# Eight float PSUM banks become six float and two bfloat16 ones in a two-layer transformer kernel

## The chip, the cores and the metric

The kernel runs on one Trainium2 chip, on its 8 cores, each core working on one of 8 sequences with no exchange between them. The time is device microseconds of the slowest core. Times of single executions of the kernel before were 11906.31 and 11831.79 us, median 11869.05 us.

## The reference

Two transformer layers over x of shape (8, 2048, 1024), each of an attention-like part and a feed-forward part, every part followed by a residual sum and a layer norm:

```python
x = L0_attn_x
x = _layernorm(x + _L0_attn_ref(x, ...), axis=-1)   # RWKV: k, v, r projections, scan over time, output projection
x = _layernorm(x + _L0_ffn_ref(x, ...), axis=-1)    # 1024 -> 4096 -> 4096 -> 4096 -> 1024, ternary weights
x = _layernorm(x + _L1_attn_ref(x, ...), axis=-1)   # gated linear attention, 4 heads, 8-bit/ternary quantised linears
x = _layernorm(x + _L1_ffn_ref(x, ...), axis=-1)    # 1024 -> 4096, depthwise conv over 3, silu, 4096 -> 1024, quantised
```

The part on which the change bears most is the recurrence of the gated linear attention:

```python
def step(S, inp):
    qt, kt, vt, gt = inp
    S = jnp.exp(gt)[..., None] * S + kt[..., None] * vt[..., None, :]
    o = jnp.einsum('bhk,bhkv->bhv', qt, S)
    return (S, o)
```

## The kernel before, in words

Each core keeps its sequence transposed in SBUF as `XA` (128 partitions, 8 channel groups, 2048 tokens, float). The program is a list of operations written out by hand, one list for each engine (`t` TensorE, `v` VectorE, `s` ScalarE, `g` GpSimd, `y` SyncE). `P.op(engine, fn, after=[...])` appends an operation and the tokens it waits for; an engine works through its list strictly in the order in which the list was written, so an operation that waits holds up all behind it. Waits become semaphore waits. The order in which the loops emit operations is therefore the order of the work.

PSUM is used as eight tensors `PS[0]` to `PS[7]`, each one bank (128 x 512 float). `PSB[b]` is the same bank b seen as 128 x 1024 bfloat16 by a bitcast. `bank_free[b]` holds the token of the last read of bank b.

The stages in order:

- `_emit_prepass`: reads the weights of layer 1, takes the mean magnitude (a matmul with ones into `PS[7]`, `t_scale`, L408), quantises them and writes them back to DRAM. It is spread in small pieces over the stages up to the first layer norm.
- `stage_l0attn`: banks 0 to 4.
- `stage_ln` (4 times): for 16 tiles of 128 tokens, 8 transposes into banks 5 and 6 (L643), two ScalarE copies out of them, statistics, and for the first three norms 8 transposes back through banks 3 and 4.
- `stage_l0ffn`: two halves of 1024 tokens. Phase A: for 32 output blocks j, 16 matmuls with `w1R` and 16 with `w2R` (L775) into four banks; Silu of the first pair on ScalarE (L785), its product with the second pair on VectorE (L795). Output block j uses banks (j % 2) * 2 + {0, 1} and 4 + (j % 2) * 2 + {0, 1}: two sets of four, in turn. There are two weight buffers; both loads of block j + 1 are issued by GpSimd when the last matmul of block j is done. Phases B and C (L823): 64 matmuls for each of 32 blocks, banks 4 to 7 in two pairs in turn, Gelu on ScalarE (L834). Then `w3R` (L860), banks 0 to 3 in two pairs.
- `stage_l1attn`: 8 blocks of 256 tokens. Transposes of x through banks 5 and 6 (L962), five quantised projections (their operand transposed as bfloat16 through banks 5 and 6, L1037, and matmuls into banks 0 to 3), then two chunks of 128 tokens with 4 heads each, then the output projection `owT` (L1397). One head of one chunk is the piece that matters here, 8 x 2 x 4 = 64 times:
  - VectorE ends its preparation with f7 (`KG`, L1240);
  - TensorE forms the 128 x 128 scores in `PS[2]` (`amm`, L1247, two matmuls of float, four instructions); VectorE masks them out of there into `A2` (`aev`, L1251);
  - TensorE transposes `KG` into `PS[4]` (`ktp`, L1257, two transposes); VectorE copies that to `KGt` (`kev`, L1260);
  - TensorE forms the output in `PS[3]` (`omm`, L1267 from the state S, then L1271 from `A2`) and the state's increment in `PS[6]` and `PS[7]` (`dmm`, L1276);
  - VectorE updates S (`su`, L1282, twice) and gates the output (`oev`, L1288); the next head's first operation on ScalarE (f1, L1215) waits for that.
- `stage_l1ffn`: 4 quarters of 512 tokens. Each quarter starts with 4 tiles: T(tt), 8 transposes of x into banks 5 and 6 (L1595), two VectorE copies (L1599, L1601), quantisation, and, one tile behind, S2(tt - 1), 8 bfloat16 transposes into banks 5 and 6 again (L1503) with two VectorE copies (L1509). Then matmuls with `f1T` (L1638) into banks 0 and 1, the convolution, a maximum over transposes through `PSB[5]` (L1683), small transposes through `PS[6]` (L1703), quantisation, matmuls with `f2T` (L1740) into banks 2 and 3.

Of the kernel before, what the change touches and what calls it, by code (L numbers as in the profile page):

```python
# [9 lines left out]
BF16 = mybir.dt.bfloat16  # L10
AF = mybir.ActivationFunctionType
ALU = mybir.AluOpType
AXX = mybir.AxisListType.X
# [185 lines left out]
def build(upto="all", tap=None):  # L199
# [47 lines left out]
    with ExitStack() as es:  # L247
# [4 lines left out]
        P = Prog(nc, sems)  # L252

        def sb(name, shape, dt=F32, stack=None):
# [11 lines left out]
              for b in range(8)]  # L266
        PSB = [PS[b][:, :].bitcast(BF16) for b in range(8)]
# [100 lines left out]
def _emit_prepass(P, pre, din, qscr, SCL, ONES, PS, d_ones):  # L368
# [4 lines left out]
    for nm, di, do in QW:  # L373
        wi = QWI[nm]
# [32 lines left out]
        def t_scale(wi=wi, inv_n=inv_n):  # L407
            mm = P.op("t", lambda t: t.matmul(  # L408
                PS[7][:, 0:1], ONES[:], pre["acc"][:, :], start=True, stop=True),
                after=[state["g"], d_ones, state["tread"]])  # L410
            state["tread"] = P.op("v", lambda v: v.tensor_scalar(
                SCL[:, wi:wi + 1], PS[7][:, 0:1], inv_n, 1e-5,
# [202 lines left out]
def stage_ln(ctx, which, toks):  # L615
# [5 lines left out]
    with ExitStack() as st_:  # L621
# [12 lines left out]
        for tt in range(NTT):  # L634
# [4 lines left out]
            for c in range(NC):  # L639
                bank = 5 + c // 4  # L640
# [7 lines left out]
                tmb[:, 0:512], PS[5][:, :], AF.Identity), after=[tps[3], stt, tm_free[sl]])  # L648
            e2 = P.op("s", lambda s, tmb=tmb: s.activation(
                tmb[:, 512:1024], PS[6][:, :], AF.Identity), after=[tps[7], e1])  # L650
# [64 lines left out]
def stage_l0ffn(ctx, toks, debug_stop=None):  # L715
# [3 lines left out]
    with ExitStack() as st_:  # L719
# [31 lines left out]
        for hb in range(2):  # L751
# [10 lines left out]
            for j in range(32):  # L762
# [19 lines left out]
                for s2 in range(2):  # L782
                    scj = j
                    bank = (j % 2) * 2 + s2
# [21 lines left out]
            for phase, nm, scoff, SRC, DST in (  # L806
                    ("B", "h1R", 64, H0, H1X), ("C", "h2R", 96, H1X, H0)):
                for j in range(32):
# [21 lines left out]
                    for s2 in range(2):  # L830
                        off = s2 * 512
                        bank = 4 + (j % 2) * 2 + s2
# [50 lines left out]
def stage_l1attn(ctx, toks):  # L883
# [6 lines left out]
    with ExitStack() as st_:  # L890
# [62 lines left out]
        for blk_i in range(8):  # L953
            t0 = blk_i * 256
            for tt in range(2):
                tps = []
                for c in range(NC):
                    bank = 5 + c // 4
# [6 lines left out]
                for half in range(2):  # L965
                    bank = 5 + half
# [155 lines left out]
            for tt in range(2):  # L1122
# [47 lines left out]
                    PSB[2][0:16, 0:128], QSz[:, 0:16], IDB[:]), after=[u7, bank_free[2]])  # L1170
                zb_free[0] = tp
                ev = P.op("v", lambda v, tt=tt: v.tensor_copy(
                    X2Q[:, tt * 128:(tt + 1) * 128], PSB[2][0:16, 0:128]),
                    after=[tp, vt])
                vt = ev
                bank_free[2] = ev
# [24 lines left out]
            for cn in range(2):  # L1201
# [12 lines left out]
                for h in range(4):  # L1214
# [49 lines left out]
                    bank_free[4] = kev  # L1264
# [10 lines left out]
                    for j in range(2):  # L1275
                        dmm.append(P.op("t", lambda t, h=h, cn=cn, j=j: t.matmul(  # L1276
                            PS[6 + j][:, :], KGt[:, j, :],
                            V[:, cn, h * 512:(h + 1) * 512],
                            start=True, stop=True),
                            after=[kev, bank_free[6 + j]]))  # L1280
                    for j in range(2):
                        su = P.op("v", lambda v, h=h, j=j: v.scalar_tensor_tensor(  # L1282
                            S[:, 2 * h + j, :], S[:, 2 * h + j, :],
                            DC[:, 2 * h + j:2 * h + j + 1], PS[6 + j][:, :],
                            ALU.mult, ALU.add), after=[dmm[j], omm, dc1, vt])
                        vt = su
                        bank_free[6 + j] = su
# [230 lines left out]
def stage_l1ffn(ctx, toks):  # L1518
# [5 lines left out]
    with ExitStack() as st_:  # L1524
# [52 lines left out]
        for q in range(4):  # L1577
# [8 lines left out]
            for tt in range(4):  # L1586
# [3 lines left out]
                for c in range(NC):  # L1590
                    bank = 5 + c // 4
# [292 lines left out]
```

How the kernel before makes its waits and increments, by code:

```python
            def body(eng):  # L145
                seen = {}
                for i, rec in enumerate(prog.ops[e]):
                    for kind, val in rec["waits"]:
                        if seen.get(kind, 0) >= val:
                            continue
                        eng.wait_ge(prog.sems[kind], val)
                        seen[kind] = val
                    inst = rec["fn"](eng)
                    if rec["dma"] is not None:
                        inst.then_inc(prog.sems[rec["dma"]], 16)
                    amt = incs[e].get(i)
                    if amt:
                        inst.then_inc(prog.sems[e], amt)
```

## Time and profile before

| | |
|---|---|
| median of 2 runs | 11869.05 us (11831.79 to 11906.31) |
| the profiled execution | 11890.16 us |
| its span (slowest core, core 7) | 11888.6 us |
| spans of all cores | 11784.2 to 11888.6 us |
| busy: TensorE (PE), VectorE (DVE), ScalarE (ACT), GpSimd (POOL) | 5393.1, 3384.1, 1840.5, 387.2 us |
| share of the span | 45%, 28%, 15%, 3% |
| the chain that ended last, by engine | PE 42%, DVE 24%, DMA 19%, issue 7%, ACT 6% |
| HBM | 70 GB/s over the span |

How to read it: the profile was taken in one execution, which was 21 us above the median of the two timed ones. Its span runs from the first to the last instruction of the slowest core. An engine's busy share is an average over stages whose limits differ. The chain that ended last is followed back from the last instruction, at each step to what released it. In the views quoted below PE is TensorE's matmuls, PEld its weight loads (which may run under the matmuls before them), and L1257 is line 1257 of the kernel.

### The profile page before, as it was taken

The page shows a single profiled execution, that of the slowest core. Times are in us where ns is not written, and L with a number is a line of the kernel's source. Part 1 is how long each engine was busy: PE and PEld are TensorE (multiplying, and loading weights), DVE is VectorE, ACT ScalarE, POOL GpSimd, SP SyncE. Part 2 cuts the span into 40 slices and gives each one's busy share as a digit, 9 for nine tenths or more (in the row PEclk, how much of TensorE's full clock was granted, in tenths as well). Part 3 has the DMA queues.
Part 4 walks back from the last instruction along what each step waited for, and adds up shares of the span by engine and source line. Part 5 has one row for each costly group of instructions (what it writes and reads, how often), then busy time and mean ns, then how long its engine had stood idle before and what let it go on. Part 6 is the DMA issues. An engine that isn't in the chain of part 4 may idle for free.

```text
span 11888.6 us, 72155 instructions; the slowest of 8 cores (11784.2 to 11888.6 us)
## 1 busy us (share of the span) xinstructions
PE 5393.1 (45%) x22678; PEld 2580.6 (22%) x22678; DVE 3384.1 (28%) x5916; ACT 1840.5 (15%) x2558; POOL 387.2 (3%) x777
## 2 busy tenths in 40 slices
PE   3430006666666666666663333333333333324323
PEld 1120002222222222222222222222222222112112
DVE  6762231000000100000004444444434434453453
ACT  1222101000000000000003122122122223121121
POOL 0000110000000000000000000000000000000000
PEclk7665558888888788878786666666666666657656
DMA  4223432222222222222211111111201101011012
GB/s 117 74 76 112 135 117 39 41 43 43 43 43 45 38 41 43 43 39 43 43 36 57 36 54 61 53 37 61 68 37 60 60 22 34 28 30 57 26 31 80
DMA packets 169144, 637.24 MB, mean 54 GB/s; under 512 B 24832, under 2 KB 25216, under 8 KB 157504
## 3 DMA queue, kind: packets, MB, share of 16 engines
q0 software_dynamic: 81088, 237.61, 10.7%
q1 hardware_dynamic: 87680, 395.02, 10.0%
q8 instruction: 187, 3.06, 0.1%
q14 instruction: 189, 1.55, 0.0%
HBM read 794.50 MB, written 42.01 MB: 70 GB/s over the span
## 4 chain that ended last, share of the span: by engine, by line
PE 42%; DVE 24%; DMA 19%; issue 7%; ACT 6%; DVEq 1%; POOL 1%; ACTq 0%; SPq 0%; POOLq 0%
PE ps L823 17%; PE ps L775 5%; DMA f_wj<-h1R 4%; DMA f_wj<-h2R 4%; PE ps L1740 2%; PE ps L1100 2%; PE ps L860 2%; DMA f_wj<-w1R 2%; PE ps L1638 2%; PE ps L1267 2%; PE ps L1397 2%; DMA pre_in<-f1T 1%; DMA pre_in<-f2T 1%; PE ps L1081 1%; DMA b_wj<-q_f2T 1%
## 5 line engine op out<-in xcount | busy, mean ns | idle before, releaser
L823 PE MATMUL ps<-f_h,f_wj 128*128 128x512 bf16 x8192 | 2059.6, 419 | 1122.6 <-DMA f_wj<-h1R 561.4
L823 PEld LDWEIGHTS ps<-f_h,f_wj 128*128 128x128 bf16 x8192 | 865.6, 106 | 2316.6 <-issue 1582.3
L871 DVE SCALAR_TENSOR_TENSOR XA<-ps,SVEC,XA 128x512 f32<-128x512 f32 x32 | 24.0, 751 | 3549.6 <-PE ps L860 3547.3
L775 PE MATMUL ps<-f_h,f_wj 128*128 128x512 bf16 x2048 | 579.6, 453 | 525.6 <-DMA f_wj<-w1R 518.6
L834 ACT ACTIVATE f_h<-ps,f_sc 128x512 bf16<-128x512 f32 x256 | 176.4, 689 | 2957.1 <-PE ps L823 2944.9
L1740 PE MATMUL ps<-b_hc,b_wj 128*128 128x512 bf16 x1024 | 293.4, 457 | 486.7 <-DVE b_hc L1472 360.6
L775 PEld LDWEIGHTS ps<-f_h,f_wj 128*128 128x128 bf16 x2048 | 230.6, 113 | 874.1 <-issue 721.3
L1100 PE MATMUL ps<-a_wl,a_xqf 128*128 128x512 bf16 x1024 | 294.9, 458 | 143.3 <-DMA a_wl<-q_vwT 63.8
L795 DVE SCALAR_TENSOR_TENSOR f_h<-ps,f_sc,f_g 128x512 bf16<-128x512 f32 x128 | 96.1, 751 | 783.1 <-ACT f_g L785 776.4
L860 PE MATMUL ps<-f_h,f_wj 128*128 128x512 bf16 x1024 | 255.5, 416 | 139.2 <-DMA f_wj<-w3R 139.2
L1247 PE MATMUL ps<-a_qg,a_kp 128*128 128x128 f32 x256 | 76.3, 454 | 524.0 <-DVE a_kg L1240 524.0
L1683 PE MATMUL ps<-c_idb,b_hc 128*128 128x128 bf16 x512 | 75.1, 302 | 523.8 <-ACT b_hc L1666 397.8
L535 PE MATMUL ps<-l_xk,l_wk 128*128 128x512 bf16 x256 | 105.5, 586 | 354.6 <-DVE l_xr L521 189.7
L408 PE MATMUL ps<-pre_acc,c_ones 128*128 128x1 f32 x18 | 4.3, 307 | 574.4 <-POOL pre_acc L401 574.4
L1740 PEld LDWEIGHTS ps<-b_hc,b_wj 128*128 128x128 bf16 x1024 | 114.0, 114 | 670.4 <-issue 595.5
L1397 PE MATMUL ps<-a_oqf,a_wl 128*128 128x128 bf16 x2048 | 185.4, 277 | 143.4 <-DMA a_wl<-q_owT 129.8
L1037 PE MATMUL ps<-c_idb,a_qz 128*128 128x128 bf16 x320 | 40.5, 306 | 460.9 <-DVE a_qz L1027 460.9
L395 ACT ACTIVATE pre_in<-pre_in 128x1024 f32<-128x1024 f32 (+1 forms) x137 | 138.0, 1008 | 667.4 <-DMA pre_in<-f2T 265.0
L1638 PE MATMUL ps<-b_xq,b_wj 128*128 128x512 bf16 x1024 | 232.0, 388 | 8.1 <-DMA b_wj<-q_f1T 4.1
L693 PE MATMUL ps<-c_idf,ln_tm 128*128 128x128 f32 x384 | 93.1, 424 | 310.0 <-DVE ln_tm L674 310.0
L1267 PE MATMUL ps<-a_S,a_qg 128*128 128x512 f32 x256 | 215.7, 993 | 0.0
L1397 PEld LDWEIGHTS ps<-a_oqf,a_wl 128*128 128x128 bf16 x2048 | 180.7, 130 | 149.5 <-issue 149.5
(345 smaller groups left out, 7374.4 us busy)
## 6 DMA issues: line engine op xcount, KB each, us to landing
f_wj<-h1R POOLq DMA_DIRECT2D x128, 512.0 KB, 6.5
f_wj<-h2R POOLq DMA_DIRECT2D x128, 512.0 KB, 6.7
a_wl<-q_owT SPq DMA_DIRECT2D x32, 2048.0 KB, 7.4
b_wj<-q_f2T SPq DMA_DIRECT2D x80, 512.0 KB, 4.6
pre_in<-f1T SPq DMA_DIRECT2D x64, 512.0 KB, 4.4
pre_in<-f2T SPq DMA_DIRECT2D x64, 512.0 KB, 3.8
a_wl<-q_vwT SPq DMA_DIRECT2D x16, 2048.0 KB, 7.4
a_wl<-q_gwT SPq DMA_DIRECT2D x16, 2048.0 KB, 7.3
```

The lines of the kernel that those rows point to most:

```text
L395: s1 = P.op("s", lambda s: s.activation(buf[0:rr, 0:cc], buf[0:rr, 0:cc], AF.Abs, accum_out=red[0:rr, :]), after=[ld, state["s"], state["r ...
L535: mmK = P.op("t", lambda t, c=c, i=i, bk=bk: t.matmul(PS[bk][:, :], WK[:, i, c * 128:(c + 1) * 128], XK[:, i, :], start=(i == 0), stop=(i ...
L775: t.matmul(PS[bank][:, :], wb[:, i, :], XB[:, i, s2 * 512:(s2 + 1) * 512], start=(i == 0), stop=(i == NC - 1)),
L823: off=off, SRC=SRC: t.matmul(PS[bank][:, :], wb[:, i2, :], SRC[:, i * 1024 + off:i * 1024 + off + 512], start=(i == 0), stop=(i == 31)),
L834: DST=DST: s.activation(DST[:, j * 1024 + off:j * 1024 + off + 512], PS[bank][:, :], AF.Gelu, scale=SC[:, scoff + j:scoff + j + 1]),
L860: off=off: t.matmul(PS[bank][:, :], wb[:, i2, :], H0[:, i * 1024 + off:i * 1024 + off + 512], start=(i == 0), stop=(i == 31)),
L1081: mm = P.op("t", lambda t, i=i, j=j, bank=bank: t.matmul(PS[bank][:, 0:256], WLv[:, i, j * 128:(j + 1) * 128], XQF[:, i, :], start=(i == 0 ...
L1100: t.matmul(PS[bank][:, :], XQF[:, i, tt * 128:(tt + 1) * 128], WLv[:, i, ds * 512:(ds + 1) * 512], start=(i == 0), stop=(i == NC - 1)),
L1267: omm = P.op("t", lambda t, h=h, j=j: t.matmul(PS[3][:, :], QG[:, j, :], S[:, 2 * h + j, :], start=(j == 0), stop=False), after=[f3, bank_ ...
L1397: cc=cc: t.matmul(PS[bank][:, cc * 128:(cc + 1) * 128], WLv[:, i, jj * 128:(jj + 1) * 128], OQF[:, rnd * 8 + i, :], start=(rnd == 0 and i ...
L1638: mm = P.op("t", lambda t, slot=slot, i=i, j=j, bank=bank: t.matmul(PS[bank][:, :], FWJ[slot][:, i, :], XQ3[:, i, :], start=(i == 0), stop ...
L1740: t.matmul(PS[bank][:, :], FWJ[s_][:, i2, :], HC[:, i, :], start=(i == 0), stop=(i == 31)),
```

## The change

Six float banks `PS[0]` to `PS[5]` are declared, and two tensors of 128 x 1024 bfloat16, `PSH[0]` and `PSH[1]`, each one bank long. `PSB[5]` and `PSB[6]` are these two; no other `PSB` exists, and `PSB[5]` is no longer the same memory as `PS[5]`. All uses of the banks are renumbered to fit:

- the float transposes of x (in the norms, at the start of each block of layer 1's attention and of each quarter of its feed-forward) go through `PS[0]` and `PS[1]`;
- phase A of `stage_l0ffn` has one set of four banks in place of two; phases B and C use banks 2 to 5 in two pairs;
- in the head, `ktp` writes `PS[2]`, the bank from which `aev` reads, and waits for `aev`; `dmm` writes `PS[4]` and `PS[5]`;
- the small transposes of layer 1's feed-forward go through `PS[4]`, the prepass's matmul through `PS[5]`, and the 16-row transposes of the gate through `PSB[5]`.

```diff
         PS = [es.enter_context(nc.psum_tensor(f"ps{b}", [128, 512], F32))
-              for b in range(8)]
-        PSB = [PS[b][:, :].bitcast(BF16) for b in range(8)]
+              for b in range(6)]
+        PSH = [es.enter_context(nc.psum_tensor(f"psh{b}", [128, 1024], BF16))
+               for b in range(2)]
+        PSB = [None, None, None, None, None, PSH[0][:, :], PSH[1][:, :], None]
...
@@ _emit_prepass: t_scale
-                PS[7][:, 0:1], ONES[:], pre["acc"][:, :], start=True, stop=True),
+                PS[5][:, 0:1], ONES[:], pre["acc"][:, :], start=True, stop=True),
...
@@ stage_ln
-                bank = 5 + c // 4
+                bank = c // 4
...
@@ stage_l0ffn, phase A: matmuls, Silu, product
-                            bank = wsel * 4 + (j % 2) * 2 + s2
+                            bank = wsel * 2 + s2
...
-                    bank = (j % 2) * 2 + s2
+                    bank = s2
...
-                    bank = 4 + (j % 2) * 2 + s2
+                    bank = 2 + s2
...
@@ stage_l0ffn, phases B and C: matmuls and Gelu
-                                bank = 4 + (j % 2) * 2 + s2
+                                bank = 2 + (j % 2) * 2 + s2
...
@@ stage_l1attn, float transposes of x
-                    bank = 5 + c // 4
+                    bank = c // 4
...
@@ stage_l1attn, gate
-                    PSB[2][0:16, 0:128], QSz[:, 0:16], IDB[:]), after=[u7, bank_free[2]])
+                    PSB[5][0:16, 0:128], QSz[:, 0:16], IDB[:]), after=[u7, bank_free[5]])
...
@@ stage_l1attn, head
-                            PS[4][:, j * 128:(j + 1) * 128], KG[:, j, :], IDF[:]),
-                            after=[f7, bank_free[4]] if j == 0 else []))
+                            PS[2][:, j * 128:(j + 1) * 128], KG[:, j, :], IDF[:]),
+                            after=[f7, aev, bank_free[2]] if j == 0 else []))
...
-                        KGt[:, :, :], PS[4][:, 0:256].rearrange("p (c n) -> p c n", c=2)),
+                        KGt[:, :, :], PS[2][:, 0:256].rearrange("p (c n) -> p c n", c=2)),
...
-                            PS[6 + j][:, :], KGt[:, j, :],
+                            PS[4 + j][:, :], KGt[:, j, :],
...
@@ stage_l1ffn, float transposes of x
-                    bank = 5 + c // 4
+                    bank = c // 4
...
-                bank_free[5] = e1
-                bank_free[6] = e2
+                bank_free[0] = e1
+                bank_free[1] = e2
```

## Rows read from the trace of the kernel before

**Rows 1.** The page's first line

```profile
span 11888.6 us, 72155 instructions; the slowest of 8 cores (11784.2 to 11888.6 us)
```

**Rows 2.** The page, chain that ended last, by line

```profile
PE ps L823 17%; PE ps L775 5%; DMA f_wj<-h1R 4%; DMA f_wj<-h2R 4%; PE ps L1740 2%; PE ps L1100 2%; PE ps L860 2%; DMA f_wj<-w1R 2%; PE ps L1638 2%; PE ps L1267 2%; PE ps L1397 2%; DMA pre_in<-f1T 1%; DMA pre_in<-f2T 1%; PE ps L1081 1%; DMA b_wj<-q_f2T 1%
```

**Rows 3.** Groups by line and form: busy us, mean ns, idle before, releasers

```profile
L823 PE MATMUL ps<-f_h,f_wj 128*128 128x512 bf16 x8192 | 2059.6, 419 | 1122.6 <-DMA f_wj<-h1R 561.4 <-DMA f_wj<-h2R 561.2
L775 PE MATMUL ps<-f_h,f_wj 128*128 128x512 bf16 x2048 | 579.6, 453 | 525.6 <-DMA f_wj<-w1R 518.6 <-DVE f_h L756 6.9
```

**Rows 4.** Timeline, phase A: start us, us, engine, line, count [idle before <-releaser]

```profile
2007.08 1.47 ACT L785 ACTIVATE f_g<-ps,f_sc 128x512 bf16<-128x512 f32 x2 [12.47 <-PE ps L775]
2007.48 0.53 POOL L81 DMA_DIRECT2D f_wj<-w1R  x1 [12.88 <-PE ps L775]
...
2008.72 1.60 DVE L795 SCALAR_TENSOR_TENSOR f_h<-ps,f_sc,f_g 128x512 bf16<-128x512 f32 x2 [12.33 <-ACT f_g L785]
...
2011.31 8.75 PE L775 MATMUL ps<-f_h,f_wj 128*128 128x512 bf16 x32 [4.44 <-DMA f_wj<-w1R]
```

**Rows 5.** Groups by line and form, operations of the head

```profile
L1251 DVE TENSOR_TENSOR a_a<-ps,c_triu 128x128 f32<-128x128 f32 x64 | 18.7, 292 | 98.5 <-PE ps L1247 94.7 <-PE ps L1257 3.7
L1215 ACT ACTIVATE a_qg<-a_gt 128x256 f32<-128x256 f32 x64 | 26.7, 418 | 491.6 <-DVE a_og L1288 490.1
```

**Rows 6.** Timeline of one head, the second of the first block

```profile
6600.78 0.42 DVE L1240 TENSOR_TENSOR a_kg<-a_et,a_k 128x256 f32<-128x256 f32 x1 [0.67 <-ACT a_et L1236]
6601.31 0.93 PEld L1247 LDWEIGHTS ps<-a_qg,a_kp 128*128 128x128 f32 x4 [6.06 <-issue]
6601.35 1.19 PE L1247 MATMUL ps<-a_qg,a_kp 128*128 128x128 f32 x4 [5.27 <-DVE a_kg L1240]
6602.12 0.44 PEld L1257 LDWEIGHTS ps<-c_idf,a_kg 128*128 128x128 f32 x2
6602.33 0.64 PE L1257 MATMUL ps<-c_idf,a_kg 128*128 128x128 f32 x2
...
6602.72 0.29 DVE L1251 TENSOR_TENSOR a_a<-ps,c_triu 128x128 f32<-128x128 f32 x1 [1.52 <-PE ps L1247]
6602.76 3.62 PE L1267 MATMUL ps<-a_S,a_qg 128*128 128x512 f32 x4
...
6607.21 1.88 PE L1276 MATMUL ps<-a_v,a_kgt 128*128 128x512 f32 x4
...
6608.40 1.60 DVE L1282 SCALAR_TENSOR_TENSOR a_S<-a_S,a_dc,ps 128x512 f32<-128x512 f32 x2 [4.84 <-PE ps L1276]
...
6610.95 0.42 ACT L1215 ACTIVATE a_qg<-a_gt 128x256 f32<-128x256 f32 x1 [10.28 <-DVE a_og L1288]
```

**Rows 7.** Windows in two heads: from:to, length, PE busy (count), clock, DMA, GB/s

```profile
6723.00:6725.90 2.90, 2.75 (x8) 0.50 0.00 0
6726.00:6731.40 5.40, 3.73 (x9) 1.00 0.00 0
7006.50:7012.60 6.10, 5.93 (x12) 0.50 0.00 0
7012.80:7016.50 3.70, 2.04 (x5) 1.00 0.00 0
```

**Rows 8.** Timeline of ACT, the first operation after these two heads

```profile
6731.59 0.42 ACT L1215 ACTIVATE a_qg<-a_gt 128x256 f32<-128x256 f32 x1 [9.12 <-DVE a_og L1288]
...
7016.72 0.42 ACT L1215 ACTIVATE a_qg<-a_gt 128x256 f32<-128x256 f32 x1 [10.83 <-DVE a_og L1288]
```

**Rows 9.** Timeline, fourth tile of the first quarter of layer 1's feed-forward

```profile
9912.22 1.01 PE L1503 MATMUL ps<-c_idb,b_q2z 128*128 128x128 bf16 x8 [7.43 <-DVE b_q2z L1495]
9912.98 0.95 DVE L1509 COPY b_xq<-ps 128x512 bf16<-128x512 bf16 x2 [0.91 <-PE ps L1503]
...
9913.56 1.94 PE L1595 MATMUL ps<-c_idf,XA 128*128 128x128 f32 x8 [0.32 <-DVE b_xq L1509]
9914.82 0.69 DVE L1599 CAST b_q2z<-ps 128x512 bf16<-128x512 f32 x1 [0.88 <-PE ps L1595]
```

More of the change, by code:

```diff
@@ L647, in stage_ln @@
             e1 = P.op("s", lambda s, tmb=tmb: s.activation(
-                tmb[:, 0:512], PS[5][:, :], AF.Identity), after=[tps[3], stt, tm_free[sl]])
+                tmb[:, 0:512], PS[0][:, :], AF.Identity), after=[tps[3], stt, tm_free[sl]])
             e2 = P.op("s", lambda s, tmb=tmb: s.activation(
-                tmb[:, 512:1024], PS[6][:, :], AF.Identity), after=[tps[7], e1])
+                tmb[:, 512:1024], PS[1][:, :], AF.Identity), after=[tps[7], e1])
             stt = e2
@@ L831, in stage_l0ffn @@
                         off = s2 * 512
-                        bank = 4 + (j % 2) * 2 + s2
+                        bank = 2 + (j % 2) * 2 + s2
                         ev = P.op("s", lambda s, j=j, off=off, bank=bank, scoff=scoff,
@@ L965, in stage_l1attn @@
                 for half in range(2):
-                    bank = 5 + half
+                    bank = half
                     ev = P.op("v", lambda v, tt=tt, half=half, bank=bank: v.tensor_copy(
@@ L1276, in stage_l1attn @@
                         dmm.append(P.op("t", lambda t, h=h, cn=cn, j=j: t.matmul(
-                            PS[6 + j][:, :], KGt[:, j, :],
+                            PS[4 + j][:, :], KGt[:, j, :],
                             V[:, cn, h * 512:(h + 1) * 512],
                             start=True, stop=True),
-                            after=[kev, bank_free[6 + j]]))
+                            after=[kev, bank_free[4 + j]]))
                     for j in range(2):
@@ L1703, in stage_l1ffn @@
                     tpu = P.op("t", lambda t, COLS=COLS, tt=tt: t.transpose(
-                        PS[6][0:1, 0:128], COLS[:, tt:tt + 1], IDF[:]),
-                        after=[vt, s4_, bank_free[6]])
+                        PS[4][0:1, 0:128], COLS[:, tt:tt + 1], IDF[:]),
+                        after=[vt, s4_, bank_free[4]])
                     evu = P.op("v", lambda v, ROW=ROW, tt=tt: v.tensor_copy(
-                        ROW[:, tt * 128:(tt + 1) * 128], PS[6][0:1, 0:128]),
+                        ROW[:, tt * 128:(tt + 1) * 128], PS[4][0:1, 0:128]),
                         after=[tpu, vt])
                     vt = evu
-                    bank_free[6] = evu
+                    bank_free[4] = evu
                 bmm = P.op("t", lambda t, ROW=ROW: t.matmul(
-                    PS[6][:, :], ONE1[:], ROW[:, 0:512],
-                    start=True, stop=True), after=[vt, bank_free[6], o1])
+                    PS[4][:, :], ONE1[:], ROW[:, 0:512],
+                    start=True, stop=True), after=[vt, bank_free[4], o1])
                 bev1 = P.op("v", lambda v, which=which: v.tensor_copy(
-                    (UB if which == 0 else WB)[:, 0:512], PS[6][:, :]),
+                    (UB if which == 0 else WB)[:, 0:512], PS[4][:, :]),
                     after=[bmm, vt])
                 bev = P.op("v", lambda v, which=which: v.tensor_copy(
-                    (UB if which == 0 else WB)[:, 512:1024], PS[6][:, :]),
+                    (UB if which == 0 else WB)[:, 512:1024], PS[4][:, :]),
                     after=[bev1])
                 vt = bev
-                bank_free[6] = bev
+                bank_free[4] = bev
             vt, gt, stt = _act_quant_fm(P, HC[:, :, :].rearrange("p c n -> p (c n)"),
@@ L1772, in stage_l1ffn @@
             after=[et1, vt])
-        et3 = P.op("t", lambda t: t.transpose(PS[6][0:1, 0:32], CL[0:32, 0:1],
-                                              IDF[0:32, 0:32]), after=[et2, bank_free[6]])
+        et3 = P.op("t", lambda t: t.transpose(PS[4][0:1, 0:32], CL[0:32, 0:1],
+                                              IDF[0:32, 0:32]), after=[et2, bank_free[4]])
         et4 = P.op("v", lambda v: v.reduce_max(
-            CL[0:1, 1:2], PS[6][0:1, 0:32], axis=AXX), after=[et3])
+            CL[0:1, 1:2], PS[4][0:1, 0:32], axis=AXX), after=[et3])
         et5 = P.op("v", lambda v: v.tensor_scalar(
@@ L1783, in stage_l1ffn @@
             CL[0:1, 5:6], CL[0:1, 2:3], 1.0 / 127, None, ALU.mult), after=[et7])
-        eb1 = P.op("t", lambda t: t.matmul(PS[6][:, 0:2], ONE1[0:1, :],
+        eb1 = P.op("t", lambda t: t.matmul(PS[4][:, 0:2], ONE1[0:1, :],
                                            CL[0:1, 4:6], start=True, stop=True),
-                   after=[et8, bank_free[6]])
-        eb2 = P.op("v", lambda v: v.tensor_copy(CL[:, 8:10], PS[6][:, 0:2]),
+                   after=[et8, bank_free[4]])
+        eb2 = P.op("v", lambda v: v.tensor_copy(CL[:, 8:10], PS[4][:, 0:2]),
                    after=[eb1])
-        bank_free[6] = eb2
+        bank_free[4] = eb2
         bank_free[5] = et2
```

16 lines of the change are left out of this document (8 added, 8 removed).

## The prediction

> **What bounds the kernel now.** I read first the page's line on the spans [rows 1]: all cores lie within 1%, so the slowest speaks for the program. Then the page's chain that ended last, by line [rows 2]: no line of layer 1 has over 2% of it; L823 of the first feed-forward has 17%, L775 has 5%, the loads of `f_wj` beside them as much again. Then the groups by line [rows 3]: at L823 and L775 TensorE is busy for 2640 us and idle before them for 1648 us, nearly all of it for weights. So in the first feed-forward the weight load is what a block waits for, not a bank. In layer 1 the chain passes from engine to engine, and there a new wait can land on the path. The change moves no data and adds no arithmetic: it changes only which operation waits for which. So I go through the places where a bank got a new neighbour, and ask in each which wait ends last.
>
> **Phase A of the first feed-forward: one set of banks in place of two.** The reader is to see in [rows 4] one change of block. The last matmul of block j ends near 2007.0; Silu reads its pair until 2008.55, the product reads the other pair until 2010.32. GpSimd issues the next loads from 2007.48 on, and TensorE resumes at 2011.31, released by the load. With one set, the first matmuls of block j + 1 wait for the Silu (done 2.76 us before they start anyway), and those with `w2R`, half a burst of 8.75 us later, for the product (done 0.99 us before the burst even begins). The loads themselves wait for the last matmul only, and that isn't moved. Cost 0, and the cover is the 4.44 us that TensorE waits for weights. If the cover were gone, block j + 1 would wait from the end of the matmuls to the end of the product, 2010.32 - 2007.08 = 3.24 us, 64 times: 207 us.
>
> Phases B, C and `w3R` keep two pairs in turn, so nothing changes but numbers. At the seams (A to B, C to `w3R`, `w3R` to the second half) the first block's banks were last read either long before or by the operation for which that block waits already. Cost 0.
>
> **The head of the gated attention: a wait of TensorE for VectorE.** This is the one added wait that I find uncovered. [rows 6] is one head. `KG` is ready at 6601.20; the scores (L1247) start 0.15 us later; the transposes of `KG` follow them with no gap, their weight load at 6602.12; only at 6602.72 does VectorE start to mask the scores (L1251, 0.29 us), while TensorE is already on L1257 and L1267. Now L1257 writes the same bank and waits for the mask. It ends at 6602.72 + 0.29 = 6603.01. From an end on VectorE to TensorE's weight load the same rows show 0.11 us (6601.20 to 6601.31 for L1247). So L1257's load starts at 6603.12 in place of 6602.12: **1.00 us later**.
>
> Who queues behind: on TensorE the four instructions of L1267, those of L1271 and the four of L1276, in this order, though only L1257 needs the wait. Behind L1276 stand the two updates of S (L1282), the gate (L1288), and behind that the next head's first ScalarE operation (L1215), with no slack anywhere: 6608.40 is released by L1276, 6610.95 by L1288. The copy L1260 gets later by the same, but its first reader is L1276, which starts 4.88 us after L1257 (6607.21 - 6602.33); hidden. The head happens 64 times [rows 5], strictly one after another, since L1215 waits for the head before it. Next to it, `owT` and the other weights are issued behind other events of the same core and simply shift. So 64 x 1.00 = **+64 us**.
>
> **The clock in the head.** L1267 and L1276 are both four instructions of 128x512 float; the first took 3.62 us, the second 1.88 us [rows 6]. The clock rises inside the head: in [rows 7] one head has it at 0.50 (1.2 GHz) until about 2.9 us after its first matmul and then at 1.00 (2.4 GHz), another until 6.1 us; until then TensorE had been busy 2.75 of 2.90 and 5.93 of 6.10 us, almost without a gap. The change cuts a gap of about 0.8 us into just this stretch. Two bounds, per head. If the rise comes at the same time as before, 1.00 us of matmuls moves behind it and takes 1.88/3.62 of its time there: -0.48 us, 64 times -31. If the busy stretch counts anew from the gap on, the rise is later against the work by the 0.98 us between the starts of L1247 and L1257: +0.47 us, 64 times +30. I see nothing that prefers one, and take the middle, 0.
>
> The Trainium skill, page "TensorE: Matmul & The Clock Gate", section "A second HAM failure mode: psum-queue depth-cycling", says that small idle gaps of TensorE between groups, from cycling through PSUM banks, make the clock fall and rise again, at a loss of throughput. Section "Part 4: PE-mode transpose" adds that transposes do not keep the clock up as matmuls do. The trace agrees so far as it shows TensorE without gaps before each rise; no row has a gap there. By this rule the rise comes later than I take it; that is the first rival.
>
> **The quarters of the last feed-forward: a wait removed.** T(tt) shared its banks with S2(tt - 1). In [rows 9] S2's transposes end at 9913.23, but T starts at 9913.56, released by the first VectorE copy, and VectorE then sits idle 0.88 us before L1599. With T in banks 0 and 1 it can start 0.3 to 0.5 us sooner and VectorE follows. Only the third and fourth tile of each quarter have S2 just ahead, 8 places: **-4 us** (at most the whole 0.88, -7; at least 0).
>
> **The rest at nothing.** The norms, the blocks' transposes of x, the prepass's matmul and the small transposes change banks whose last readers were done, and VectorE or ScalarE work released them before and after. `bank_free[5]` now serves two different banks, but all its tokens are at least one phase old when they are waited for. Bounds here: 0 to +2.
>
> **Sum.** +64 - 4 = **+60 us**. Against the profiled execution of 11890.16 us that is 11950; that execution was 21 us above the median of the runs, 11869.05. On the median: **11929 us**, +0.5%. A measurement of this kernel tells about 2% (237 us) from no change, so this would read as no change.
>
> **Rivals.**
> - *The clock comes much later or not at all in the head.* For it: the gap lies where there was none. From [rows 8] and [rows 5]: ScalarE's wait from head to head is 490.1/48 = 10.21 us in the mean, 9.12 in the head with the early rise, 10.83 in that with the late one. All heads late: (10.83 - 10.21) x 64 = +40, total +100, 11969 us. If it never rose, the parts at 1.00, 2.04 to 3.73 us busy [rows 7], would take 1.93 times as long: +1.9 to +3.5 us, some 2.7 in the mean, 64 times 170, total +230, 12099 us. Against: after the gap 5 us and more of unbroken matmuls remain.
> - *The wait costs little.* The mask starts sooner, or the clock falls in step: all heads with the early rise give (9.12 - 10.21) x 64 = -70, total -10, 11859 us. The rise at the same time gives +28, 11897 us.
> - *Phase A is exposed* (slower). Mechanism: a block waits for the readers of the only set. Place L775, price 207 us, total +267, 12136 us. It decides only from where the wait for weights (4.44 us) falls under about 1.5 us, the Silu's reach; nothing shortens the load.
> - *The view does something else.* If instructions on a native bfloat16 tensor took another time than on the bitcast, reads as L1509 would show it. A float read of the same width takes 0.69 us against about 0.42 [rows 9], 256 such copies (160 + 64 + 32 by the loops): 69 us either way. Against: the rows call both operands bf16 already; the instruction is the same.
>
> **How the numbers follow.** My forecast, the gap on the path and the clock between its bounds: 70%, own range +28 to +92, 11897 to 11961 us. Clock much later: 13%, of which at most 2 reach over +237 with other mishaps. Wait costs little, -10 to +28: 11%. Phase A exposed: 2%. The view or anything unseen: 4%, half of it up. Two runs of before lie 75 us apart, so I widen my own range by about 35 us at both ends, to 11862 and 11996, which takes in the near halves of the first two rivals. Range 11865 to 12000 us. Slower by over 2%: 0.03; faster by over 2%: 0.01; within 2%: 0.96.
>
> **What would show it.** L1257's weight load released by L1251, in all 64 heads, about 1.0 us later against L1247 than now; L1215's mean wait near 11.2 us in place of 10.21 (over 11.8: the clock; under 10.7: the second rival). Idle time before L775 still some 526 us and released by loads; if part of it goes to L785 or L795, the third rival. L1595 no longer released by L1509. Wrong most easily: the clock's rise in the head, which I put at neutral only between two bounds.

## The result and the profile after

| | before | after |
|---|---|---|
| median of the timed runs | 11865.37 us | 11923.25 us |
| lowest to highest | 11823.63 to 11978.02 | 11896.3 to 11959.83 |
| span of the profiled execution, slowest core | 11888.6 us | 11916.8 us |
| mean span of the 8 cores in it | 11834 us | 11890 us |

The ratio is 1.005, 95% interval 1.0034 to 1.0066: 58 us slower (40 to 78), surely slower but by far less than 2%. The forecast was 11929 us and "no change that a measurement tells".

The spans of the slowest cores differ by 28 us only, the mean over the cores by 56 us, as the medians do. In some executions, of either kernel, cores of one die show a granted clock of 0.81 for part of the time and end late; the ratios leave out those that lost over about 1% by it, and stages are read below on cores without it where it matters.

One head of the gated attention, the last of the first chunk, against [rows 6]; timeline of the changed kernel (start us, us, engine, line, count, idle time before and what ended it). Lines are 2 higher than before:

```profile
6602.92 0.42 DVE L1242 TENSOR_TENSOR a_kg<-a_et,a_k 128x256 f32<-128x256 f32 x1 [0.67 <-ACT a_et L1238]
6603.46 0.93 PEld L1249 LDWEIGHTS ps<-a_qg,a_kp 128*128 128x128 f32 x4 [6.04 <-issue]
6603.49 1.19 PE L1249 MATMUL ps<-a_qg,a_kp 128*128 128x128 f32 x4 [5.25 <-DVE a_kg L1242]
6604.86 0.29 DVE L1253 TENSOR_TENSOR a_a<-ps,c_triu 128x128 f32<-128x128 f32 x1 [1.51 <-PE ps L1249]
6605.26 0.29 PEld L1259 LDWEIGHTS ps<-c_idf,a_kg 128*128 128x128 f32 x2 [0.88 <-issue]
6605.29 0.66 PE L1259 MATMUL ps<-c_idf,a_kg 128*128 128x128 f32 x2 [0.61 <-DVE a_a L1253]
6605.75 3.38 PE L1269 MATMUL ps<-a_S,a_qg 128*128 128x512 f32 x4
```

The weight load of KG's transposes starts 1.80 us after that of the scores; before it was 0.81 us. The transposes are released by the mask (L1253), and the state's matmuls (L1269) follow behind them as before. The weight load now starts 0.03 us before its transposes, before it was 0.21 us. L1269 starts 2.83 us after the start of `KG`'s last operation, before (L1267) it was 1.98 us: 0.85 us later.

The idle time of TensorE before the transposes, ScalarE's wait from head to head, and two stages with large loads, in the groups by line and form (busy us, mean ns, idle before, releasers):

```profile
L1259 PE MATMUL ps<-c_idf,a_kg 128*128 128x128 f32 x128 | 42.2, 433 | 40.0 <-DVE a_a L1253 40.0
L1217 ACT ACTIVATE a_qg<-a_gt 128x256 f32<-128x256 f32 x64 | 26.6, 416 | 534.0 <-DVE a_og L1290 532.5
L777 PE MATMUL ps<-f_h,f_wj 128*128 128x512 bf16 x2048 | 586.6, 457 | 525.9 <-DMA f_wj<-w1R 519.0 <-DVE f_h L758 6.9
L1399 PE MATMUL ps<-a_oqf,a_wl 128*128 128x128 bf16 x2048 | 201.8, 293 | 135.0 <-DMA a_wl<-q_owT 121.4 <-DVE a_oqf L1380 13.6
```

L1217 waits 532.5/48 = 11.09 us from head to head, before 490.1/48 = 10.21 us [rows 5]. L777, phase A, sits idle 525.9 us, all of it ended by weight loads and the first cast, as the 525.6 us of [rows 3]. L1399, the output projection, is the row that the prediction did not look at. Before, it was this:

```profile
L1397 PE MATMUL ps<-a_oqf,a_wl 128*128 128x128 bf16 x2048 | 185.4, 277 | 143.4 <-DMA a_wl<-q_owT 129.8 <-DVE a_oqf L1378 13.6
```

The same 2048 matmuls take 16 us more, with no new wait in front of them. The copies out of the banks that are now bfloat16 tensors take 425 ns, as they did before (L1509 and L1378, now L1511 and L1380).

To see where the 56 us of the mean span went I cut the timelines at the same operations in both kernels (means over the 8 cores, us):

| stage | before | after | difference |
|---|---|---|---|
| up to the first feed-forward | 1736.4 | 1735.3 | -1.1 |
| first feed-forward | 4434.2 | 4422.1 | -12.1 |
| of it phase A (first to last Silu, both halves) | 849.6 | 851.3 | +1.7 |
| attention of layer 1 | 3344.7 | 3415.8 | +71.1 |
| of it the 64 heads (KG ready to output gated) | 607.7 | 663.7 | +56.0 |
| of it the 16 output projections (first matmul to sum) | 308.7 | 323.5 | +14.8 |
| last feed-forward and last norm | 1992.2 | 1989.8 | -2.4 |

The two norms between these stages, some 160 us each, did not change and are left out. The attention is steady: its 8 cores lie within 3334.8 to 3356.3 us before and 3409.2 to 3426.0 us after. The first feed-forward is not: 4395 to 4463 us on the cores of one execution, so its -12 says nothing. The record of the clock tells why. Before, cores 4 to 7 stand at 0.81 for 192 to 209 us of the first feed-forward and for 39 to 97 us of the attention; after, cores 0 and 1 for some 200 us of the first feed-forward, half of it in phase A. On the cores without it the first feed-forward differs by +4 us and phase A by -1 us, and the attention takes 3340.0 us before and 3415.8 after, +76: the heads +57.7, the projections +16.8.

### The profile page after: what moved, and what is told of

Read it like the earlier page. It is cut to its first block, busy times and chain, and to the rows that moved or that the text cites. A ratio compares the mean times of both kernels' runs of the same rounds, so it can differ in the third digit from the quotient of the medians.

```text
span 11916.8 us, 72147 instructions; the slowest of 8 cores (11858.7 to 11916.8 us)
## 1 busy us (share of the span) xinstructions
PE 5379.6 (45%) x22678; PEld 2584.7 (22%) x22678; DVE 3384.0 (28%) x5916; ACT 1836.7 (15%) x2558; POOL 387.4 (3%) x777
## 4 chain that ended last, share of the span: by engine, by line
PE 42%; DVE 24%; DMA 19%; issue 7%; ACT 6%; DVEq 1%; POOL 1%; ACTq 0%; SPq 0%; POOLq 0%
PE ps L825 17%; PE ps L777 5%; DMA f_wj<-h2R 4%; DMA f_wj<-h1R 4%; PE ps L1742 2%; PE ps L1102 2%; PE ps L862 2%; DMA f_wj<-w1R 2%; PE ps L1640 2%; PE ps L1269 2%; PE ps L1399 2%; DMA pre_in<-f1T 2%; DMA pre_in<-f2T 1%; DMA b_wj<-q_f2T 1%; PE ps L1083 1%
## 5 line engine op out<-in xcount | busy, mean ns | idle before, releaser
L777 PE MATMUL ps<-f_h,f_wj 128*128 128x512 bf16 x2048 | 586.6, 457 | 525.9 <-DMA f_wj<-w1R 519.0
L777 PEld LDWEIGHTS ps<-f_h,f_wj 128*128 128x128 bf16 x2048 | 231.9, 113 | 880.2 <-issue 749.3
L797 DVE SCALAR_TENSOR_TENSOR f_h<-ps,f_sc,f_g 128x512 bf16<-128x512 f32 x128 | 96.1, 751 | 792.2 <-ACT f_g L787 785.6
L1685 PE MATMUL psh<-c_idb,b_hc 128*128 128x128 bf16 x512 | 75.0, 302 | 523.6 <-ACT b_hc L1668 397.5
L1399 PE MATMUL ps<-a_oqf,a_wl 128*128 128x128 bf16 x2048 | 201.8, 293 | 135.0 <-DMA a_wl<-q_owT 121.4
L1039 PE MATMUL psh<-c_idb,a_qz 128*128 128x128 bf16 x320 | 40.5, 307 | 460.8 <-DVE a_qz L1029 460.8
L1269 PE MATMUL ps<-a_S,a_qg 128*128 128x512 f32 x256 | 228.2, 1046 | 0.0
L1399 PEld LDWEIGHTS ps<-a_oqf,a_wl 128*128 128x128 bf16 x2048 | 197.2, 139 | 141.1 <-issue 141.1
```

Of the source, the lines that this page charges most:

```text
L777: t.matmul(PS[bank][:, :], wb[:, i, :], XB[:, i, s2 * 512:(s2 + 1) * 512], start=(i == 0), stop=(i == NC - 1)),
L1269: omm = P.op("t", lambda t, h=h, j=j: t.matmul(PS[3][:, :], QG[:, j, :], S[:, 2 * h + j, :], start=(j == 0), stop=False), after=[f3, bank_ ...
L1399: cc=cc: t.matmul(PS[bank][:, cc * 128:(cc + 1) * 128], WLv[:, i, jj * 128:(jj + 1) * 128], OQF[:, rnd * 8 + i, :], start=(rnd == 0 and i ...
```

## The experiments

Times of whole kernels scattered by up to 4% on some of the chips on which these ran, the kernel before among them. Where the interval is wide, the verdict below rests on the stage durations of the trace, taken as in the table above, on the cores named.

**KG's transposes in a bank of their own (e1_own_bank)**

```diff
-                            PS[2][:, j * 128:(j + 1) * 128], KG[:, j, :], IDF[:]),
-                            after=[f7, aev, bank_free[2]] if j == 0 else []))
+                            PS[0][:, j * 128:(j + 1) * 128], KG[:, j, :], IDF[:]),
+                            after=[f7, bank_free[0]] if j == 0 else []))
...
-                    bank_free[2] = kev
+                    bank_free[0] = kev
```

> The changed kernel with one thing undone: KG's transposes in the head go to PS[0], a bank that nobody reads at that time, and no longer wait for the mask. Theory W (the wait of TensorE for the mask carries the change): the +58 us go away. ScalarE's mean wait from head to head falls back from 532.5/48 = 11.09 us to about 10.21 us, the output projection's 16 pieces lose the 15 us in all that they gained, and the time comes to 0.9995 of the kernel before, some 11860 us. Rival S (phase A's single set of banks or the bfloat16 tensors carry it): the time stays near 1.005 of the kernel before.

Ratio to the kernel before 0.9964, interval 0.9897 to 1.0031. The attention takes 3342.9 us (3337.8 to 3347.6), the heads 606.6, the projections 307.2: the 71 us are gone to within 3 us of the 3340.0 of cores 0 to 3 before, the projections' part included. The wait from head to head is back at 486.7/48 = 10.14 us:

```profile
L1217 ACT ACTIVATE a_qg<-a_gt 128x256 f32<-128x256 f32 x64 | 26.6, 416 | 488.2 <-DVE a_og L1290 486.7
```

**That wait alone in the kernel before (e2_head_only)**

```diff
-                            PS[4][:, j * 128:(j + 1) * 128], KG[:, j, :], IDF[:]),
-                            after=[f7, bank_free[4]] if j == 0 else []))
+                            PS[2][:, j * 128:(j + 1) * 128], KG[:, j, :], IDF[:]),
+                            after=[f7, aev, bank_free[2]] if j == 0 else []))
...
-                    bank_free[4] = kev
+                    bank_free[2] = kev
```

> The kernel before with one part of the change alone: KG's transposes go to the bank of the scores and wait for the mask. Theory W: +56 us in the 64 heads and some +15 us in the output projections behind them, 1.006 of the kernel before (11935 us), with TensorE idle 40 us before the transposes, released by VectorE. Rival S: under +15 us, 1.001 or less.

Ratio 1.0074, interval 1.0011 to 1.0137. Attention 3413.6 us, +69 against before; heads 663.3, projections 321.3. TensorE is idle before the transposes as in the changed kernel, to the tenth:

```profile
L1257 PE MATMUL ps<-c_idf,a_kg 128*128 128x128 f32 x128 | 42.2, 434 | 40.0 <-DVE a_a L1251 40.0
```

One wait carries the whole change of the attention to within some 2 us; nothing that these runs can tell is left there for the other renumberings or for the bfloat16 tensors.

**One set of banks in phase A alone (e3_one_set)**

```diff
-                            bank = wsel * 4 + (j % 2) * 2 + s2
+                            bank = wsel * 2 + s2
...
-                    bank = (j % 2) * 2 + s2
+                    bank = s2
...
-                    bank = 4 + (j % 2) * 2 + s2
+                    bank = 2 + s2
```

> The kernel before with one part of the change alone: phase A of the first feed-forward uses one set of four banks in place of two. Theory C (the wait for weights covers the readers of the banks): 0 us, TensorE's idle time before its matmuls stays at about 526 us and is released by the weight loads, none of it by Silu or the product. Rival S: up to 207 us, 64 times 3.24 us; any third of that would show as +70 us, 1.006.

Ratio 1.0035, interval 0.999 to 1.008, which alone would allow up to 90 us. The trace is sharper. Phase A takes 852.4 us against 849.6, within the 848 to 863 us of its own cores. The 863 are those of cores 4 and 5, which stand at 0.81 for 114 to 118 us of it; without them phase A is 0.6 us shorter than before. TensorE's waits before it are the same, with no release by Silu or product:

```profile
L775 PE MATMUL ps<-f_h,f_wj 128*128 128x512 bf16 x2048 | 594.3, 462 | 524.1 <-DMA f_wj<-w1R 517.2 <-DVE f_h L756 6.9
```

**The quarters' transposes alone (e4_tiles_only)**

```diff
-                    bank = 5 + c // 4
+                    bank = c // 4
...
-                    Zb[:, 0:512], PS[5][:, :]), after=[tps[3], vt, zb_free[tt % 2]])
+                    Zb[:, 0:512], PS[0][:, :]), after=[tps[3], vt, zb_free[tt % 2]])
```

> The kernel before with one part of the change alone: the float transposes T of the last feed-forward go to PS[0] and PS[1]. Theory: each of the third and fourth tiles of a quarter starts 0.3 to 0.5 us sooner, -4 us in all, seen only in the trace: VectorE's idle time before L1599 falls by some 4 us and no transposes of T are released by L1509. Rival: VectorE is no sooner at T's copies and nothing changes (0 us).

VectorE's idle time before L1599, in the view of that line, before and with the edit (us, times):

```profile
L1599 DVE CAST b_q2z<-ps x8: 691/691/693, 9893.4 to 11300.7; 128x512 bf16<-128x512 f32 x8
its engine sat idle before it (us, times) until:
  PE ps L1595: 7.8, 9
```

```profile
L1599 DVE CAST b_q2z<-ps x8: 690/692/693, 9821.5 to 11224.4; 128x512 bf16<-128x512 f32 x8
its engine sat idle before it (us, times) until:
  PE ps L1595: 3.4, 8
```

-4.4 us, the same on all 8 cores, and in the changed kernel too. Of so small a term only such a row can tell; the whole kernel can't.

**Same bank, other order (e7_state_first)**

In the changed kernel the two matmuls of the state, which read neither the mask nor KG, are written ahead of KG's transposes:

```diff
+                    omm = None
+                    for j in range(2):
+                        omm = P.op("t", ... PS[3], QG[:, j, :], S[:, 2 * h + j, :] ...)
                     ktp = []
                     for j in range(2):
                         ktp.append(...)
...
-                    omm = None
-                    for j in range(2):
-                        omm = P.op("t", ...)
```

> The changed kernel, banks as they are, but the two matmuls of the state (L1269) are written before KG's transposes. The transposes still wait for the mask, which is done long before TensorE comes to them. Theory W (TensorE stands at the wait because of the order, not because of the bank): ScalarE's mean wait from head to head falls from 11.09 to about 10.2 us, layer 1's attention by some 70 us (from 3416 to about 3345 us, mean of the cores), the time to 0.9995 of the kernel before. Rival B (sharing the bank itself costs, whatever the order: TensorE writes while VectorE has just read): most of the 11.09 us stays.

Ratio 0.9994, interval 0.9748 to 1.0239, so undecided by time. On cores 0 to 3, without the 0.81, the attention takes 3342.4 us (before on these cores 3340.0, after 3413.7), the heads 607.5, and from head to head (core 0):

```profile
L1217 ACT ACTIVATE a_qg<-a_gt 128x256 f32<-128x256 f32 x64 | 26.6, 416 | 490.6 <-DVE a_og L1290 489.2
```

Rival B falls. With the shared bank and work that is ready ahead of the wait, the attention is as long as with a bank of its own (3342.9 us in e1_own_bank); the price was the order.

**The state's matmuls ahead of the scores too (e8_state_before_scores)**

```diff
+                    omm = None
+                    for j in range(2):
+                        omm = P.op("t", ... PS[3], QG[:, j, :], S[:, 2 * h + j, :] ...)
                     amm = None
                     for j in range(2):
                         amm = P.op("t", ...)
```

with KG's transposes in `PS[0]` as in e1_own_bank.

> The changed kernel with KG's transposes in PS[0] and the state's two matmuls written before the scores: they need only QG and S, which are there some 2.2 us before KG. Theory: TensorE starts at about 6599.1 in place of 6601.35 in the head of the rows, the mask's reader L1271 starts 1.7 us sooner, and a head shrinks by 1.7 us against the kernel before: 64 times, -110 us, ratio 0.991, attention at about 3235 us. Rival: the mask becomes the last wait before L1271 and eats most of it (under -50 us).

Ratio 0.9878, interval 0.9733 to 1.0024, so undecided by time. Attention 3217.9 us in the mean of cores 0 to 3, 3221.2 on the others: -125 us. But four of these cores stand at 0.81 for 330 to 480 us of this stage. The other four (0, 1, 6 and 7) take 3199 us, -141 against the 3340.0 of cores 0 to 3 before, and that is the fairer reading: 31 us more than the 110 expected. No run shows where they come from. The mask does become a wait before its reader, but a small one (core 3; 20.1 to 22.9 us over all cores):

```profile
L1273 PE MATMUL ps<-a_v,a_a 128*128 128x512 f32 x128 | 77.5, 689 | 21.5 <-DVE a_a L1259 21.5
```

**The projections: moving their start by 1.3 us (e9_shift_after, e10_shift_before)**

The projections' 14.8 us had no wait to their name. What differs is the clock. The first burst of a projection before and after, timeline and windows (from:to, length, PE busy, clock):

```profile
6664.85 5.20 PE L1397 MATMUL ps<-a_oqf,a_wl 128*128 128x128 bf16 x64 [0.85 <-DVE a_oqf L1378]
```

```profile
6664.85:6667.90 3.05, 3.05 (x30) 0.50 0.02 5
6668.00:6670.05 2.05, 2.05 (x36) 1.00 0.00 0
```

```profile
6640.56 6.46 PE L1399 MATMUL ps<-a_oqf,a_wl 128*128 128x128 bf16 x64 [0.85 <-DVE a_oqf L1380]
```

```profile
6640.56:6646.20 5.64, 5.64 (x54) 0.50 0.01 3
6646.50:6647.00 0.50, 0.50 (x10) 1.00 0.00 0
```

Before, the clock rose to 1.00 some 3.1 us into the burst, and about 36 of 64 matmuls ran at it; after, it rose 5.7 us in, for 10 of them. By the record of the clock, on each of cores 0 to 3 before, 8 of the 16 rises stood 2.6 to 3.2 us into the first burst and 8 stood 4.7 to 5.9 us in. After, 119 of the 128 on all cores stood 5.4 to 6.0 us in, the other 9 at 2.6. A test: compute one maximum twice between heads and projection, in both kernels.

```diff
                     hv.append(w2)
                     vt = w2
+                vt = P.op("v", lambda v: v.reduce_max(
+                    CL[:, 5:6], QSz[:], axis=AXX,
+                    apply_absolute_value=True), after=[vt])
+                hv[1] = vt
```

> The changed kernel with one VectorE maximum of 1.22 us computed twice, once in each of the 16 chunks, between the last head and the output projection. It adds 16 x 1.32 = 21 us of serial work. Theory P (the projection's two bursts got 15 us longer because the clock now rises late in each of them, 5.4 to 6.0 us after the start of the first burst in all 16): with a start 1.3 us later against the clock, the rise comes at about 4.1 to 4.7 us, the 16 first bursts lose some 10 us in all, the second some 4, so attention grows by only 5 to 10 us against the changed kernel. Rival R (the 15 us are a cost of banks or loads): attention grows by 21 us, the first bursts keep 102 us in all.

> The kernel before with the same doubled VectorE maximum of 1.22 us in each of the 16 chunks, 21 us of serial work in all. Theory P (what the added piece costs depends on when the projection's bursts start against the clock's rises): in the kernel before the rises stand 2.6 to 3.2 us after the start of some first bursts and 5.0 to 6.0 us after that of others; 1.3 us later, the first kind come too early to count and rise late, the second kind rise sooner, so the bursts stay at about 308 us in all and the attention grows by the full 15 to 25 us against the kernel before (3345 us). Rival: the attention absorbs the added piece here too, as in the changed kernel (under +8 us), which would mean that VectorE has slack between the heads and the projection.

Neither run has a ratio. In the traces cores 4 to 7 of the first and 0 to 3 of the second have no 0.81 in the attention; on them, and on the same cores of the two kernels:

| | attention | projections | first bursts |
|---|---|---|---|
| changed kernel, cores 4 to 7 | 3417.9 | 324.0 | 102.1 |
| with 16 x 1.32 us more (e9) | 3417.0 | 310.4 | 93.3 |
| kernel before, cores 0 to 3 | 3340.0 | 306.7 | 90.9 |
| with 16 x 1.32 us more (e10) | 3363.9 | 313.4 | 96.1 |

In the changed kernel 21 us of added serial work cost -0.9 us; in the kernel before they cost 23.9 us. The rises in e9's first bursts stand 4.0 to 4.7 us in, where 4.1 to 4.7 was expected; in e10's they stand 3.7 to 5.3 us in, where there were two groups before, and the bursts grew by 6.7 us where they were expected to stay. So VectorE has no slack there. What an added piece costs depends on when it makes the bursts start against the rises of the clock. I had expected 5 to 10 us in e9; the second bursts and the next heads (658.7 us against 663.9) gained as well.

**Phase A without its cover (e5_early_two_sets, e6_early_one_set)**

The first weight buffer is released after its own 16 matmuls, so the next load runs under the second half of a block. Once in the kernel before, once in the changed one:

```diff
                     wb = (wb1, wb2)[wsel]
+                    if wsel == 1:
+                        mmhalf = mmlast
...
-                wj_free[slot1] = mmlast
+                wj_free[slot1] = mmhalf
```

> The kernel before with phase A's first weight buffer released after the matmuls with w1R, not after the whole block: the load of block j + 1 then runs under the second half of block j. This takes away most of the 4.6 us of waiting between blocks that cover the readers of the banks; two sets of banks. Theory C: the wait before a block falls from 4.6 us to under 0.5 us, the two phases A shrink by some 62 x 4.2 = 260 us, ratio 0.978.

> The same earlier release in the changed kernel, which has one set of banks in phase A. Theory C (the single set was free only under the cover of the loads): now a block waits for the Silu of the block before, 1.5 us after its end, so phase A keeps 60 to 100 us more than with two sets and TensorE's idle time before L777 is ended by ScalarE. Rival F (a single set never costs, e.g. because the product and Silu are overlapped by the first matmuls anyway): the feed-forward takes as long as with two sets, within 15 us. The attention keeps its +71 us against the kernel before in either case.

Ratios 0.9747 (0.9708 to 0.9785) and 0.9832 (0.9803 to 0.9861). Phase A takes 516.3 us with two sets, 545.3 us with one; the attention 3340.6 and 3412.5 us, the same +72 as ever. The two ratios differ by 100 us of the kernel before, as these 72 and 29 add up to. Idle time before its matmuls, two sets, then one:

```profile
L777 PE MATMUL ps<-f_h,f_wj 128*128 128x512 bf16 x2048 | 460.5, 382 | 306.7 <-DMA f_wj<-w1R 257.3 <-DMA f_wj<-w2R 27.6 <-ACT f_g L787 14.3
```

```profile
L779 PE MATMUL ps<-f_h,f_wj 128*128 128x512 bf16 x2048 | 468.7, 383 | 328.6 <-DMA f_wj<-w1R 269.6 <-ACT f_g L789 50.3 <-DVE f_h L758 6.9
```

One change of block with one set, in the timeline:

```profile
1912.58 1.47 ACT L789 ACTIVATE f_g<-ps,f_sc 128x512 bf16<-128x512 f32 x2 [7.20 <-PE ps L779]
...
1913.78 7.27 PE L779 MATMUL ps<-f_h,f_wj 128*128 128x512 bf16 x32 [1.41 <-DMA f_wj<-w1R]
```

With one set, the view names Silu for 50.3 us of waits; in the kernels with the old release it named it for none. (It names it for 14.3 us with two sets too, where no block needs the Silu just before it, so the split is rough.) The set that was free now costs 29 us (32 if the two cores of the first run that stand at 0.81 in phase A are left out), not 60 to 100: the load still lands so that TensorE stands 1.41 us, Silu's first half is done by then and its second nearly, so the cover is thin but not gone. Neither theory had the size. The earlier release itself brought 333 us instead of 260: of the slowest cores some 219 us less idle time, though a wait of 1.3 us was left and not under 0.5, and 119 us less busy time. L775's matmuls went from 453 ns in the mean [rows 3] to 382 ns at the higher clock: on core 7 before, the record has 0.50 for 338 of the 852 us, with TensorE standing 4.7 us between blocks, and with the earlier release for 10 us or less on every core.

**All of it together (best1)**

The banks of the kernel before, the state's matmuls ahead of the scores, and each of the two buffers, in all phases of the first feed-forward, waited for and released by its own half:

```diff
                     for ihalf in range(2):
                         wb = WJ[wbs[ihalf]]
+                        if ihalf == 1:
+                            mmh = mm
...
-                                    after=[stok[0], stok[1], bank_free[bank], h0_done_v]
+                                    after=[stok[0], bank_free[bank], h0_done_v]
                                     if i == 0 and s2 == 0 else
+                                    [stok[1]] if i == 16 and s2 == 0 else
...
-                    wj_free[wbs[0]] = mm
+                    wj_free[wbs[0]] = mmh
```

> The kernel before, its banks, with the state's matmuls ahead of the scores and with every weight buffer of the first feed-forward (phases A, B, C and w3R) released after its own half of the matmuls and waited for by its own half. Sum of what it should bring: -125 us in the heads (measured), -260 us in phase A, and most of the 8.8 us before each of the 128 blocks of phases B and C and of the 4.4 us of w3R, but at a denser TensorE the clock may be granted lower, so of 1120 + 139 us I expect some 900: about 10600 us, ratio 0.89. If the loads can't keep up with the matmuls, the wait moves to the second half of each block and the gain is about half.

Five executions, 9832.29 to 10032.44 us, median 9950.54. The ratio, by the rule above from 9832.29 and 9845.32 alone, is 0.8335, interval 0.8314 to 0.8356: faster than the kernel before by a sixth. The first feed-forward falls from 4434 to 2570 us, the attention to 3196 us.

```profile
L827 PE MATMUL ps<-f_h,f_wj 128*128 128x512 bf16 x8192 | 1775.7, 379 | 17.3 <-DVE f_h L797 7.3 <-DMA f_wj<-h1R 4.3 <-ACT f_h L839 3.7
```

1122.6 us of waiting [rows 3] are down to 17.3. I had subtracted for a lower clock that did not come in the profiled execution (9832.29 us): these matmuls are busy for 2059.6 us before, 1775.7 now. They run at the higher clock nearly throughout: the record has 0.50 for 1398 to 1471 of the 4200 us from 1800 on before, and for 10 to 27 of the 2400 us from 1800 on now.

## Why the prediction was right

**The added wait.** Right in place and cause, and over-sized by about 9 us. The weight load of the transposes came 0.99 us later against the scores' (1.01 in the mean over all heads and cores, 1.00 predicted), released by the mask, 64 times. But the prediction took the delay of the weight load for the delay of the work. Before, that load started 0.21 us ahead of the transposes, while the scores' matmuls still ran [rows 6]; now it starts 0.03 us ahead, so the work behind it moved by 0.85 us only (0.86 in the mean), 64 times 55 us in place of 64. e2_head_only and e1_own_bank show that this wait alone makes, and its removal alone undoes, the change.

**The clock in the head.** Taken as neutral between -31 and +30 us, and close to that. The heads grew by 56.0 us (57.7 against cores 0 to 3 of before, which have no 0.81) where the work moved by 55, so the clock cost 1 to 3 us. In its records over all heads and cores the rise comes 5.0 us after KG in the mean before and 5.9 us after, about as far as the work moved. The rule of the Trainium skill (page "TensorE: Matmul & The Clock Gate", section "A second HAM failure mode: psum-queue depth-cycling"), by which such a gap should bring a loss, shows inside the head by these 1 to 3 us at most. It had a kernel with gaps in every iteration; here there is one of 0.6 us in a stretch of 9. ScalarE's mean wait, 11.09 us, was predicted near 11.2.

**The quarters.** -4 predicted, -4.4 in e4_tiles_only.

**Phase A.** 0 predicted, covered by the wait for weights. Measured +1.7 in the changed kernel and +2.8 in e3_one_set, and -1.1 and -0.6 without the cores that stand at 0.81 in it: nothing. The bound for the exposed case, 207 us, was far too high: it charged the product's end too, which is needed only half a burst later. With most of the cover gone the price was 29 us; that the Silu begins to count where the wait for weights falls under about 1.5 us fits the 1.41 us there.

**What was missed.** The output projections, +14.8 us. "The rest at nothing" held for waits but not for time: a stage behind the changed one, with the same instructions and the same waits, ran longer because its bursts started at another moment against the rises of the clock. The sum of the terms as measured is +56 + 15 - 4 = +67 us, or +58 + 17 - 4 = +71 on the cores without the 0.81, against 58 us between the medians (40 to 78 by the interval), 73 between the lowest times, and 60 predicted. So the total was better than its parts, and that was luck: a missed +15 to +17 stood against an overcounted 6 to 8, and the rest is within the interval.

One number was read carelessly. The 1648 us of idle time in the first feed-forward hold one wait of 228 us, for the first weights of all, which GpSimd issues at 1744.92, right behind its last write-back of the prepass at 1743.84; between blocks of phase A it is 4.7 us in the mean, some 290 us in all.

## What to carry to other kernels

A bank shared between two steps costs the time by which it holds up what stands behind the new wait in the engine's list, not what the wait's own reader needs: with ready work written ahead of the waiting instruction, the sharing cost nothing that could be seen here. Measure the delay at the start of that work, not at the weight load in front of it. Before a buffer is taken away, ask what covers its readers, and write down what it costs once that cover is optimised away. And a wait of TensorE for weights at each block can be worth more than it measures: here 219 us less of it came with 119 us less busy time, at the higher clock.

## What the runs showed of the hardware

The cost of a few added or removed microseconds before a burst of matmuls is not their sum. 21 us of extra serial work cost -0.9 us in one kernel and 23.9 us in its neighbour, since short bursts (5 to 6.5 us here) are either caught early by a rise of the clock from 0.50 to 1.00 (1.2 to 2.4 GHz), as the one with 36 of its 64 matmuls at the higher level, or late, as the one with 10 of 64. A stage that repeats evenly can meet the rises evenly: after the change 119 of 128 first bursts stood at the late end.

Dense matmuls on all 8 cores did not bring the clock down in the profiled execution of best1; that they never do is not shown. Windows in the first feed-forward, core 3 (from:to, length, PE busy, clock, DMA, GB/s):

```profile
1800.00:2400.00 600.00, 569.05 (x2592) 1.00 0.44 72
2400.00:3000.00 600.00, 593.88 (x2748) 1.00 0.46 75
3000.00:3600.00 600.00, 550.39 (x2483) 0.99 0.43 69
```

TensorE is busy for 92 to 99% there, and the granted clock is 0.99 to 1.00. On all 8 cores it is 0.98 to 1.00 in the windows from 1800 to 4200 us.
